# Block 0's second norm moved behind the next group's first sums, block 1's first norm moved into the seventh attention

## What is computed

```python
for n in range(STEPS):                      # 2 steps
    A = _top_p_attention(Xa, W1, W2, W3)    # softmax, kept to 90% of its mass, made stochastic
    Xf = R @ Xf
    Xa = A @ Xa
    Z = Z + Xf @ U1[n].T + Xa @ U2[n].T
h = X + Z
...                                         # L1: layernorm(h) * ln_g + ln_b
x = x + L1(...)                             # residual, this is x2
h = jnp.maximum(_layernorm(x, axis=-1), 0.0)
m_0_1 = incidence_1.T @ x_0                 # L2's first product, x_0 = h, incidence_1 = adj
```

## Time and profile before

| | us |
|---|---|
| median of 3 runs | 1078.0 |
| lowest, highest | 1077.09, 1078.36 |
| profiled execution | 1077.07 |
| its span | 1075.3 |
| busy: TensorE, VectorE, ScalarE, POOL | 842.4, 780.1, 509.8, 68.6 |

### The profile page before, as it was taken

One profiled execution on the slowest core, in us unless ns is written; L12 is line 12 of the kernel. 1 busy time (PEld: TensorE's weight loads), 2 busy tenths in 40 slices (PEclk: granted clock), 3 DMA queues, 4 the chain that ended last, 5 costly groups with the idle time before them and its releaser, 6 DMA issues.

```text
span 1075.3 us, 12282 instructions
## 1 busy us (share of the span) xinstructions
PE 842.4 (78%) x3886; PEld 567.7 (53%) x3886; DVE 780.1 (73%) x2363; ACT 509.8 (47%) x979; POOL 68.6 (6%) x68
## 2 busy tenths in 40 slices
PE   5889958886886853939779868869569899996695
PEld 4754325554665642837256546647448476553342
DVE  5968679888997998970697898798789712325715
ACT  4877235356467476413442654664775332023212
POOL 0020110000000000000000000010000101002201
PEclk9989988888998985969799789979779999998798
DMA  9949203424004000000043320140160455500001
GB/s 338 348 169 432 104 31 126 140 96 157 1 1 158 1 0 2 1 2 1 1 156 128 108 79 1 60 152 1 50 247 36 158 235 232 237 1 0 1 0 39
DMA packets 20221, 108.25 MB, mean 101 GB/s; under 512 B 1824, under 2 KB 8752, under 8 KB 9776
## 3 DMA queue, kind: packets, MB, share of 16 engines
q1 hardware_dynamic: 18752, 106.77, 26.8%
q10 hardware_dynamic: 1392, 0.61, 0.2%
HBM read 88.23 MB, written 19.14 MB: 100 GB/s over the span
## 4 chain that ended last, share of the span: by engine, by line
PE 46%; DVE 29%; ACT 12%; issue 9%; POOL 2%; DMA 1%; DVEq 1%; POOLq 0%; SPq 0%; ACTq 0%
DVE AT L1519 10%; PE PS L808 9%; PE PS L743 7%; PE PS L676 5%; PE PS L546 4%; DVE mxv L1658 4%; PE PS L877 3%; DVE nd L1522 3%; PE PS L1062 3%; PE PS L1038 3%; ACT BC L1251 3%; ACT AT L1251 2%; PE PS L1068 2%; DVE AT L2098 2%; PE PS L612 1%
## 5 line engine op out<-in xcount | busy, mean ns | idle before, releaser
L1084 ACT ACTIVATE AT<-PS 128x512 f32<-128x512 f32 (+2 forms) x240 | 118.3, 560 | 131.1 <-PE PS L546 113.9
L743 PE MATMUL PS<-K,ST 128*128 128x512 f32 x224 | 127.9, 724 | 43.5 <-ACT EA L1219 23.1
L546 PE MATMUL PS<-ident,AT 128*128 128x128 f32 x544 | 82.6, 286 | 40.2 <-DVE AT L1519 17.9
L1519 DVE SCALAR_TENSOR_TENSOR AT<-EA,se 128x2048 uint8<-128x2048 f32 (+1 forms) x46 | 107.6, 2346 | 2.5 <-PE PS L546 1.1
L743 PEld LDWEIGHTS PS<-K,ST 128*128 128x128 f32 x224 | 49.9, 234 | 105.1 <-issue 105.0
L1519 DVE SCALAR_TENSOR_TENSOR AT<-AT 128x2048 uint8<-128x2048 f32 (+2 forms) x48 | 96.1, 2002 | 2.5 <-PE PS L546 1.7
L1658 DVE TENSOR_REDUCE mxv<-PS 128x1 f32<-128x2048 f32 x32 | 73.2, 2287 | 29.7 <-PE PS L743 24.2
L546 PEld LDWEIGHTS PS<-ident,AT 128*128 128x128 f32 x544 | 66.8, 148 | 50.3 <-DVE AT L1519 18.7
L2098 DVE MAX8 AT<-AT 128x8 f32<-128x256 f32 x256 | 88.4, 412 | 0.8
L808 PE MATMUL PS<-AT 128*128 128x128 f32 x512 | 70.4, 288 | 6.3 <-ACT AT L1084 5.7
L808 PE MATMUL PS<-hr,AT 128*128 128x128 f32 x512 | 69.0, 284 | 5.6 <-ACT AT L1084 4.8
(11 more groups left out here) (297 smaller groups left out, 1475.0 us busy)
## 6 DMA issues: line engine op xcount, KB each, us to landing
AT<-keep_at SPq DMA_DIRECT2D x32, 1024.0 KB, 5.0
EA<-in_adj SPq DMA_DIRECT2D x20, 1024.0 KB, 6.6
keep_at<-AT SPq DMA_DIRECT2D x8, 2048.0 KB, 25.0
AT<-keep_at SPq DMA_DIRECT2D x8, 2048.0 KB, 12.4
AT<-in_adj SPq DMA_DIRECT2D x12, 1024.0 KB, 5.0
EA<-keep_degrees SPq DMA_DIRECT2D x1, 1024.0 KB, 6.6
keep_x<-K SPq DMA_DIRECT2D x4, 256.0 KB, 8.6
out<-EA SPq DMA_DIRECT2D x4, 256.0 KB, 2.3
```

The source lines that it names most:

```text
L546: return pe.transpose(dst, src, ident[0:p, 0:p])
L743: mm = pe.matmul(bank(half(gi, k) + n), ST[1][:, k * P:(k + 1) * P], wide_keys[:, n * BK:(n + 1) * BK], start=True, stop=True)
L1084: return act.activation(dst, src, ACT.Copy)
L1519: return dve.scalar_tensor_tensor(out=o, in0=x0, scalar=s, in1=x1, op0=op0, op1=op1, **k)
```

## The change

Before the seventh attention, in the tail of the period that attends group 5, ScalarE did: second half of block 0's norm (`second_norm(0)`), one tile of first sums, `second_scaled(0)`, two tiles of first sums, `first_norm(1)`, three tiles of second sums; and at the head of the next period `first_scaled(1)`. Now it does the three tiles of first sums, `second_norm(0)`, one tile of second sums, `second_scaled(0)`, two tiles of second sums; at the head of the next period `first_norm(1)`, and `first_scaled(1)` behind the first tile of the attention. What follows for block 1 inside that attention is one tile later: its rows are turned at tiles 2 and 3 in place of 1 and 2, and summed at tile 3 and behind it in place of tiles 2 and 3. Block 0's places inside the attention of group 5 are the same, and so is every instruction of VectorE, POOL and SP.

```diff
@@ attend, TensorE
-                if normed is not None and k in (1, 2):
-                    rows_turned(normed, k - 1)
+                if normed is not None and k - normed in (1, 2):
+                    rows_turned(normed, k - normed - 1)
...
-                if normed is not None and k in (1, 2):
-                    pe.wait_ge(ln_ts, 2 * normed + k)
-                if normed is not None and k in (2, 3):
+                if normed is not None and k - normed in (1, 2):
+                    pe.wait_ge(ln_ts, 2 * normed + k - normed)
+                if normed is not None and k - normed in (2, 3):
                     pe.wait_ge(exT_ok, G * gi + k)
-                    rows_summed(normed, k - 2)
+                    rows_summed(normed, k - normed - 2)
...
                 if k == G - 1:
                     result_turned(step, g, k)
+                    if normed == 1:
+                        pe.wait_ge(exT_ok, G * gi + k + 1)
+                        rows_summed(normed, 1)
                     projected(step, g, k)
@@ rows_turned
                 if b < 2:
-                    pe.wait_ge(z_ok, NT + G * (b + 1) + h)
+                    pe.wait_ge(z_ok, NT + G * (b + 1) + b + h)
@@ result_out, ScalarE
-                    if normed is not None and k < 2:
-                        turned_out(normed, k)
+                    if normed is not None and k - normed in (0, 1):
+                        turned_out(normed, k - normed)
...
-                    if normed is not None and k in (1, 2):
-                        summed_out(normed, k - 1)
+                    if normed is not None and k - normed in (1, 2):
+                        summed_out(normed, k - normed - 1)
@@ the loop over g, ScalarE
-                    if normed is not None:
-                        first_scaled(normed)
+                    if normed == 0:
+                        first_scaled(0)
+                    elif normed == 1:
+                        first_norm(1)
                     for k in range(G):
                         if g > 0:
                             attend(step, g - 1, k, (lambda: guess(step, g + 1)) if more and k == G - 1 else None, normed)
+                            if normed == 1 and k == 0:
+                                first_scaled(1)
...
                     if more:
+                        sums_below(step, g + 1, 0, (0, 1, 2))
+                        unit_next()
+                        if step == 1 and g == 1:
+                            first_norm(0)
                         if normed == 0:
                             second_norm(0)
-                            sums_below(step, g + 1, 0, (0,))
+                            sums_below(step, g + 1, 1, (0,))
                             second_scaled(0)
-                            sums_below(step, g + 1, 0, (1, 2))
-                        else:
-                            sums_below(step, g + 1, 0, (0, 1, 2))
-                        unit_next()
-                        if step == 1 and g > 0:
-                            first_norm(g - 1)
-                        sums_below(step, g + 1, 1, (0, 1))
+                        sums_below(step, g + 1, 1, (1,) if normed == 0 else (0, 1))
                         unit_next()
                         sums_below(step, g + 1, 1, (2,))
```

## The result

The changed kernel takes 1081.56 us (median of 13 runs, 1078.54 to 1082.30) against 1077.57 us of the kernel before (13 runs, 1075.61 to 1078.64): a ratio of 1.0036, 95% interval 1.0028 to 1.0045, so 4.0 us slower, with 3.0 to 4.8 in the interval. The forecast was 1081.5 us, 0.35% slower. The total came out. One step of its working did not: it hid two errors, which nearly cancel.

A forecast was written before the change was run, and what follows sets the result against it. VectorE and ScalarE bound before group 6's attention, TensorE after; +4.6 (start) - 1.6 (attention) + 0.5 (tail) = +3.5 us gave 1080.6, stated as 1081.5 because the median lies 0.9 above the profiled run; range 1078.9 to 1084.0.

The forecast's parts named there:

- What bounds: VectorE and ScalarE bound until group 6's attention, TensorE after; VectorE's 2.5 us gain is lost behind TensorE's queued products.
- The sums on ScalarE: First sums end at 778.5, VectorE's 2.54 us wait goes, block 0's scaling ends at 787.9 in place of 773.85.
- Start of the attention: Group 6's attention on TensorE starts behind the three products, at 801.2 in place of 796.64: +4.6 us.
- The attention: Group 6's four tiles on TensorE take 32.0 us in place of 33.6: -1.6 us; tile 0 gives back 3.2.
- tile 1's wait: At tile 1 of group 6's attention, block 1's scaling ahead of ScalarE's copies costs TensorE 1.4 us.
- The tail: Behind tile 3, ScalarE's reading of block 1's second sum delays the product of row tile 4: +0.5 us.
- Everything behind it ... shifts as a whole.: From the product of row tile 4 on, all follows TensorE and ScalarE in the old order, with no further gain or loss.
- a rival, not in the sum: Product 4 meets full clock, 1.8 us come back; part of the no-change case, +0.3 to +2 us, 16 in 100.
- 16 us in hand: VectorE has group 7's first mask nearly 16 us before TensorE asks, so about 1 us of wait there costs nothing.
- The rival in which the long idle time costs more: After 22 us idle TensorE's clock rises later at the three products: over +5 us, up to +11; 12 in 100.
- The faster rival: Block 0's scaling finished before 781, products done before the attention's release: -1.4 us, or -3.0 without tile 1's stall; 5 in 100.
- The rule weighed: Idle gaps throttle TensorE's clock; closing the gap before group 6's attention would by the rule alone be worth 3.2 us.

The follow-up runs named there:

- x_products_behind_wait: x_masks_wait with products 0 to 2 moved behind group 6's attention on TensorE; 1093.75 us, ratio 1.0148 to the kernel before.
- x_block1_back: Kernel before with the change's tail order alone, block 1's scaling and rows where they were; ratio 1.0027 to the kernel before.
- x_masks_wait: The change with VectorE's masks of group 7 held back until POOL has the root of block 2's second norm; ratio 1.0004 to the kernel before.
- v_norm_first: Kernel before with block 0's scaling behind all three first-sum tiles and block 1's scalings spread over tile 0 of the attention; 1070.35 us, ratio 0.9938.
- The two v_ kernels: v_norm_first, and the same with each product waiting only for its own scaled tile and VectorE's group 7 masks held back (1068.51 us, ratio 0.9929).
- b_wait_met: Kernel before with a VectorE wait added ahead of group 7's masks, for POOL's third root, which is long done; ratio 0.9992 to the kernel before.
- x_scaled_spread: The change with block 1's four scalings spread between ScalarE's copies of tile 0 in place of all ahead of tile 1's; ratio 1.0028 to the kernel before.

## Why the prediction was right, and where it was not

- **What bounds.** Right. The reciprocal came 2.5 us earlier and TensorE took it 4.4 us later. x_products_behind_wait shows that it was the queue.
- **The sums on ScalarE.** Right within 0.1 us: VectorE's wait gone, the scaling of block 0 starts at 787.75, which less the mark's shift of 1.38 is 786.4, as reckoned.
- **Start of the attention.** +4.6 forecast, +4.41 measured. The products took 13.06 and not 13.26 (12.90 and not 13.1 from their start to the attention's), and their start was as reckoned.
- **The attention.** -1.6 forecast. From its start to product 3 it took 31.78 us in place of 33.63, so -1.85. Tile 0: 5.89 for 5.9; tile 1's wait: 1.49 us in the trace; tile 1 took 7.91, forecast 8.0.
- **The tail.** +0.5 forecast, +0.66 measured (product 4 at +3.22, product 3 at +2.56). To here the sum is right: +3.5 forecast, +3.2 measured, and by x_block1_back and x_masks_wait more of it is block 1's later steps (2.0) than the late products (1.2 net).
- **"Everything behind it ... shifts as a whole."** This is the step that failed, twice, with opposite signs. Product 4 ran at full clock, -1.7 us, in both traces of this order (after and x_masks_wait); the text had it as a rival, not in the sum. And POOL's root for block 2 took 2.0 us longer, since VectorE's masks now ran where POOL worked. They came 4.35 us earlier from the mark, 2.25 by VectorE's own earlier work and 2.1 by a shorter wait that stays unexplained, and the root came 1.5 us later. I had costed VectorE's earlier arrival at nothing, with 16 us in hand on its own path, and never asked whose operations its masks would meet. At the attention of group 7: +3.2 - 1.7 + 2.0 = +3.5.
- **Luck.** That these two come to +0.3 together is luck. The total also hangs on how the time is read: from the mark to the end of the trace the change costs 3.4 us, in the medians 4.0, and 3.6 to 4.2 with the masks held back in both kernels, where POOL's 2.0 us are gone. Which part of the medians is which, from product 4 on, stays open.
- **The clock.** The price of a start at the low clock was no higher behind 22 us (13.06 us for the products) than behind 8 (13.26), and tile 0 gave back its 3.2 us, as x_block1_back isolates (4.40 less 1.21). The rival in which the long idle time costs more did not come.
- **The faster rival.** Its condition did not come true here, but its sum was too small: it gave tile 0 only 1 us for products done before the release. v_norm_first, which meets that condition, has tile 0 at 5.95 us, 3.1 less than before.
- **The rule weighed.** What TensorE: Matmul & The Clock Gate (the Trainium skill) would credit to closing the gap was there: tile 0 at 5.89 us for 9.09. The two v_ kernels have it without paying by a late start.

## What to carry to other kernels

Ask of delayed work not only who waits for it, but what stands behind it in its engine's queue. The three products were off the path until they came late, and then held all of it. And large operations of an engine with slack can move, by time gained or by a wait of their own that changes: look at what they slow there, GpSimd above all, and try to hold the slack one back if the other is on the path. Give the kernel before the same hold, or its worth will be booked to the change. The best of the orders tried here was the one that ended the fill-in work just when the release came.

## What the runs showed of the hardware

- GpSimd operations of 0.19 or 0.20 us took 0.50 to 2.02, and one of 1.01 took 3.00, when they started beside VectorE's 128x2048 masks; held apart, they took 0.19, 1.01 and 0.20. In six traces the short ones ended 0.04 to 0.07 us behind the end of the mask that they met, and in three the 1.01 us one ended 0.86 to 0.87 us behind. The Trainium skill has a rule that would give this in SBUF — State Buffer, in the section on the two sides: a VectorE operation with two SBUF inputs and a GpSimd operation that reads SBUF take a shared port pair as an exclusive lock for the whole instruction. The rows agree that GpSimd waits for the mask in hand, with 2.0 us as the cost at TensorE in the trace. They do not show the reverse: a mask that began inside the 1.01 us operation (before, and b_wait_met) kept its 2.35 us. Whether the masks count as two inputs (their scalar apart, in0 and in1 are the same row) no run here asked.
- One and the same eight records, product 4, took 3.67, 5.37, 6.63 and 6.74 us in the traces of before, the change and its parts, whose starts differ by up to 3.2 us from the mark, behind 2.5 to 3.15 us without work. Where the order up to there was the same, so was the time, to 0.01 us (5.37 in the four traces with the order of the kernel before, 6.63 and 6.62, 3.67 twice), but between x_scaled_spread and the change 1.3 us of shift went with 3.1 us of time. A difference of that size between two orders can be the clock alone, so positions ahead of such a place say more than the end.
